# One fused transformer layer on one core: a sixth gate/up product ahead of the gate, the first query ahead of a cast, casts moved round a table load, and a twelfth split down

## The reference

```
x = x + xattn(layernorm(x), ctx_512)       # 16 heads, causal mask over the first 32 context rows
x = x + attn(layernorm(x))                 # 16 heads, q/k/v/o with LoRA of rank 16
x = x + ffn(layernorm(x))

def ffn(flat):                             # 128 x 256; E = 32 experts, I = 128, top 4
    scores = sqrt(softplus(flat @ router_w.T))
    _, idx = top_k(scores + expert_bias, 4)
    topv   = scores at idx, divided by their sum
    out = sum over all experts e of  p[:, e] * swiglu(flat, gate_w[e], up_w[e], down_w[e])
    return out + swiglu(flat, shared_gate_w, shared_up_w, shared_down_w)

def swiglu(x, wg, wu, wd):
    g = clip(x @ wg.T, -7, 7);  u = clip(x @ wu.T, -7, 7)
    return silu(g) * u @ wd.T
```

## Time and profile before

| | |
|---|---|
| three runs, us | 77.66, 73.18, 72.33 (median 73.18) |
| profiled execution, us | 72.22 |
| its span, first to last instruction, us | 70.4 |
| granted TensorE clock, mean | 1.000 |
| busy: TensorE, GpSimd, VectorE, ScalarE | 93%, 77%, 67%, 65% |
| HBM traffic | 15.52 MB read |

### The profile page before, as it was taken

The page is one execution under the profiler, slowest core; times in us unless marked ns, Lnnn a source line. Parts: engine busy times, 40 slices in busy tenths (PEclk is TensorE's granted clock), DMA queues, the critical chain, the costliest instruction groups (busy, mean ns, idle before and its releaser), DMA issues.

```text
span 70.4 us, 1578 instructions
## 1 busy us (share of the span) xinstructions
PE 65.3 (93%) x542; PEld 48.5 (69%) x542; DVE 47.0 (67%) x133; ACT 46.0 (65%) x101; POOL 54.2 (77%) x60
## 2 busy tenths in 40 slices
PE   5999989999799999999989999999999999999940
PEld 2348647789564496467666878888887888788820
DVE  0089488486497536499999945679955887697440
ACT  0606375876998654769979899999668851275220
POOL 7430003889999996998799999999999999999000
PEclk9999999999999999999999999999999999999999
DMA  0998999999999999999999995200000000000002
GB/s 3 271 297 245 329 425 404 291 328 419 417 419 403 393 401 407 396 383 388 393 407 400 391 372 201 76 0 0 0 9 0 0 0 0 0 0 0 0 0 74
DMA packets 6343, 15.75 MB, mean 224 GB/s; under 512 B 704, under 2 KB 1472, under 8 KB 6336
## 3 DMA queue, kind: packets, MB, share of 16 engines
q1 hardware_dynamic: 6048, 15.39, 59.2%
q10 hardware_dynamic: 288, 0.27, 1.1%
HBM read 15.52 MB, written 0.13 MB: 222 GB/s over the span
## 4 chain that ended last, share of the span: by engine, by line
PE 52%; DMA 16%; DVE 14%; SPq 7%; ACT 4%; issue 3%; DVEq 0%; ACTq 0%
DMA gu_raw<-moe_w_dram 16%; PE bP L591 16%; PE bY L624 7%; PE bY L613 6%; PE bXT L603 5%; SPq L275 4%; PE bE L591 4%; DVE gu_clip L964 4%; PE bY L626 3%; SPq L283 2%; DVE h L1018 2%; PE bP L419 2%; PE bXT L448 1%; PE bXT L641 1%; PE bY L444 1%
## 5 line engine op out<-in xcount | busy, mean ns | idle before, releaser
L349 POOL TENSOR_TENSOR gu_w<-gu_raw,gu_w 128x512 fp32r<-128x512 f32 x27 | 33.7, 1277 | 0.6 <-ACT gu_w L705 0.6
L591 PE MATMUL bP<-gu_w,xnT_parts 128*128 128x512 f32 x66 | 18.6, 417 | 0.0
L591 PEld LDWEIGHTS bP<-gu_w,xnT_parts 128*128 128x128 f32 x66 | 12.2, 188 | 2.9 <-issue 0.5
L1018 DVE SCALAR_TENSOR_TENSOR h<-gu_clip,gate,bP 128x128 f32<-128x128 f32 x26 | 7.8, 344 | 5.2 <-ACT bP L790 5.2
L964 DVE TENSOR_SCALAR gu_clip<-bP,clip_at 128x512 f32<-128x512 f32 x13 | 10.4, 806 | 1.1 <-PE bP L591 1.1
L355 POOL TENSOR_TENSOR gu_w<-dn_w,gu_w 128x512 fp32r<-128x512 f32 x8 | 10.1, 1285 | 0.0
L698 ACT ACTIVATE gu_w<-gu_raw 128x1024 fp32r<-128x1024 f32 x9 | 9.4, 1048 | 0.3 <-issue 0.3
L796 ACT ACTIVATE hT_parts<-bXT 128x256 fp32r<-128x256 f32 x11 | 4.2, 383 | 7.1 <-PE bXT L603 7.1
L705 ACT ACTIVATE gu_w<-gu_raw 128x512 fp32r<-128x512 f32 x10 | 6.1, 621 | 1.2 <-DMA gu_raw<-moe_w_dram 1.2
L603 PE MATMUL bXT<-consts_sb,h 128*128 128x128 f32 x33 | 6.5, 277 | 0.3 <-DVE h L1018 0.2
L790 ACT ACTIVATE bP<-gu_clip,rstd 128x256 f32<-128x256 f32 x13 | 6.1, 472 | 0.4 <-DVE gu_clip L964 0.4
(11 more groups left out here) (161 smaller groups left out, 124.8 us busy)
## 6 DMA issues: line engine op xcount, KB each, us to landing
gu_raw<-moe_w_dram SPq DMA_DIRECT2D x16, 512.0 KB, 9.6
dn_w<-moe_w_dram SPq DMA_DIRECT2D x16, 256.0 KB, 9.5
aw_sb<-attn_w_dram SPq DMA_DIRECT2D x2, 512.0 KB, 7.4
shared_sb<-shared_w_dram SPq DMA_DIRECT2D x1, 416.0 KB, 14.9
small_sb<-small_dram SPq DMA_DIRECT2D x1, 338.0 KB, 7.3
xwq_sb<-x_wq_dram SPq DMA_DIRECT2D x1, 256.0 KB, 3.5
lora_sb<-lora_dram SPq DMA_DIRECT2D x1, 256.0 KB, 4.7
ctx_sb<-ctx_kv_dram ACTq DMA_DIRECT2D x1, 192.0 KB, 3.2
```

What stands on the lines that cost most here:

```text
L349: nc.gpsimd.tensor_tensor(gu_w[:, gu_slot(p), 1, cols], gu_raw[:, raw_slot(p), cols], gu_w[:, gu_slot(p), 0, cols], ALU.subtract).then_inc ...
L591: last = nc.tensor.matmul(bGU[n % 5][:, 0:GU], xnT_parts[:, a, k, :], gu_w[:, gu_slot(n - 1), w, k * GU:(k + 1) * GU], start=(k == 0 and a ...
L1018: last = nc.vector.scalar_tensor_tensor(h[:, n % 4, e], gu_clip[:, n % 4, e, 1, :], weight_e, bank[:, e * 2 * I:e * 2 * I + I], ALU.mult, ...
```

## The change

Five edits, in one kernel.

1. **A sixth product ahead of the gate.** `BANKS` = 6: products 3 to 6 are issued before the first transposes, product 7 behind T(0). Product 6 gets the bank `bXT1` (`bOnce`). The routing scratch moves from there to `bShared`. Until unit 6 all transposes use the one bank `bXT0`, so `transpose_h(n)` waits for the copy of n - 1 and not of n - 2, and from the first split unit on for its low part as well. How far products are ahead is now `ahead(n)`: n + 6, from turn 5 on n + 5, from turn 8 on n + 4.
2. **Unit 0.** Its silu goes to the bank of unit 1 rather than the shared one, and `gate_h(0)` waits for silu 1.
3. **The first query of the second attention** is copied before the next cast rather than behind it, and the cast of pair 5 (counted from 0) is done in two halves, the second behind the copy of the probabilities.
4. **Casts round the table load.** The cast of pair 9 is done whole ahead of the table load; that of pair 10 in two halves behind silu 1. The copy of the leftover column moves up in the routing chain.
5. **Twelve split downs.** `LAST` = 12, `FIRST` = 4. A down cast is placed in the turn in which the product of its slot is issued.

```diff
+BANKS = 6
+LEADS = (5, 8)
-LAST = 11
+LAST = 12
+def ahead(n):
+    return min(n + BANKS - sum(n >= at for at in LEADS), PAIRS)
...
-        bHT = (bXT1, bXT0)
-        bGU = (bP[0][:, 0], bP[0][:, 1], bP[1][:, 0], bP[1][:, 1], bE)
+        bOnce = bXT1
+        def bGU(n):
+            if n == BANKS:
+                return bOnce
+            return (bP[0][:, 0], bP[0][:, 1], bP[1][:, 0], bP[1][:, 1], bE)[(n if n < BANKS else n - 1) % 5]
+        def bHT(n):
+            return bXT0 if n <= BANKS or n % 2 == 0 else bXT1
...
-                if n > 5:
-                    pe.wait_ge(h_ready, n - 4)
+                if n > BANKS:
+                    pe.wait_ge(h_ready, n - BANKS + (1 if n < 2 * BANKS else 2))
...
                 pe.wait_ge(h_ready, n + 1)
-                if n >= 2:
-                    pe.wait_ge(hT_ready, n - 1)
-                if n - 2 > FIRST:
-                    pe.wait_ge(hT_low_ready, n - 2 - FIRST)
+                back = 1 if n <= BANKS else 2
+                if n >= back:
+                    pe.wait_ge(hT_ready, n - back + 1)
+                if n - back > FIRST:
+                    pe.wait_ge(hT_low_ready, n - back - FIRST)
...
-            for n in range(WHOLE + 1, 6):
+            for n in range(WHOLE + 1, BANKS + 1):
                 gate_up(n)
             transpose_h(0, width=1)
+            gate_up(BANKS + 1)
             transpose_h(1)
             for n in range(2, PAIRS + 1):
-                if n + 4 <= PAIRS:
-                    gate_up(n + 4)
+                if ahead(n) > ahead(n - 1):
+                    gate_up(ahead(n))
                 transpose_h(n)
...
             for c in range(DC):
-                gu_high_chunk(WHOLE + 2, c)
                 act.wait_ge(q_psum, DC + c + 1)
                 nc.scalar.activation(qT[:, 1, c], ...)
+                gu_high_chunk(WHOLE + 2, c)
-            gu_high(WHOLE + 3)
+            gu_high_chunk(WHOLE + 3, 0)
...
             copy_probsT(1)
+            gu_high_chunk(WHOLE + 3, 1)
             gu_high(WHOLE + 4)
...
             nc.scalar.activation(root[:], half_power[:], ACT.Exp, scale=0.5).then_inc(root_ready, 1)
+            gu_high(WHOLE + 7)
             nc.scalar.preload_act_table(ACT.Silu)
...
-            gu_high_chunk(WHOLE + 7, 0)
             silu_unit(0)
             silu_unit(1)
-            gu_high_chunk(WHOLE + 7, 1)
-            gu_high(EARLY)
+            for c in range(DC):
+                gu_high_chunk(EARLY, c)
...
                 for i in range(UNITS, LAST):
-                    if dn_from(i) + 1 == n + 4:
+                    if ahead(n - 1) <= dn_from(i) < ahead(n):
                         dn_high(i)
```

More of the change, by code:

```diff
@@ L176, in build @@
         bLogits = bShared[:, 2 * I:SHARED]
-        logits_n, den, inv_root = (bXT1[:, at:at + E] for at in (64, 128, 192))
-        score2, weight = (bXT1[:, at:at + E + 1] for at in (256, 320))
-        bHT = (bXT1, bXT0)
+        logits_n, den, inv_root = (bShared[:, at:at + E] for at in (288, 320, 352))
+        score2, weight = (bShared[:, at:at + E + 1] for at in (384, 448))
         bLast = bP[0][:, 0]
-        bGU = (bP[0][:, 0], bP[0][:, 1], bP[1][:, 0], bP[1][:, 1], bE)
+        bOnce = bXT1
[5 more added lines that the diff above has]
+            return bXT0 if n <= BANKS or n % 2 == 0 else bXT1
         ld = {n: sem("ld_" + n) for n in ("x", "consts", "mask", "small", "ctx", "xwq", "lora", "rows", "aw_kq", "aw_vo", "shared")}
@@ L590, in gate_up @@
                         for a, w in HI_LO:
-                            last = nc.tensor.matmul(bGU[n % 5][:, 0:GU], xnT_parts[:, a, k, :],
+                            last = nc.tensor.matmul(bGU(n)[:, 0:GU], xnT_parts[:, a, k, :],
                                                     gu_w[:, gu_slot(n - 1), w, k * GU:(k + 1) * GU],
@@ L597, in transpose_h @@
                 pe.wait_ge(h_ready, n + 1)
-                if n >= 2:
-                    pe.wait_ge(hT_ready, n - 1)
-                if n - 2 > FIRST:
-                    pe.wait_ge(hT_low_ready, n - 2 - FIRST)
+                back = 1 if n <= BANKS else 2
[3 more added lines that the diff above has]
+                    pe.wait_ge(hT_low_ready, n - back - FIRST)
                 for e in range(width):
-                    last = nc.tensor.transpose(bHT[n % 2][:, e * T:(e + 1) * T], h[:, n % 4, e, :], ident)
+                    last = nc.tensor.transpose(bHT(n)[:, e * T:(e + 1) * T], h[:, n % 4, e, :], ident)
                 last.then_inc(hT_psum, 1)
@@ L619, in down @@
                     if n == PAIRS:
-                        pe.wait_ge(h_ready, PAIRS)
+                        pe.wait_ge(h_ready, PAIRS + 1)
                     for e in range(2):
@@ L782, in _ @@
             nc.scalar.activation(root[:], half_power[:], ACT.Exp, scale=0.5).then_inc(root_ready, 1)
+            gu_high(WHOLE + 7)
             nc.scalar.preload_act_table(ACT.Silu)
             def silu_unit(n):
-                act.wait_ge(clip_ready, n + 1)
+                act.wait_ge(clip_ready, max(n, 1) + 1)
                 width = 2 if n else 1
-                bank = bGU[n % 5] if n else bShared
-                dst = bank[:, 0:width * 2 * I].rearrange("p (e w i) -> p e w i", e=width, w=2)[:, :, 0, :]
+                dst = bGU(max(n, 1))[:].rearrange("p (e w i) -> p e w i", e=2, w=2)
+                dst = dst[:, :, 0, :] if n else dst[:, 0:1, 1, :]
                 nc.scalar.activation(dst, gu_clip[:, n % 4, 0:width, 0, :], ACT.Silu, scale=rstd[:, 2:3]
@@ L795, in hT_unit @@
                 dst = hT[:, n % 3, 0:width] if n <= FIRST else hT_parts[:, n % 3, 0]
-                nc.scalar.activation(dst, bHT[n % 2][:, 0:width * T], ACT.Copy).then_inc(hT_ready, 1)
+                nc.scalar.activation(dst, bHT(n)[:, 0:width * T], ACT.Copy).then_inc(hT_ready, 1)
             def dn_high(i):
@@ L956, in clip @@
                 width = 2 if n else 1
-                bank = bGU[n % 5] if n else bShared
+                bank = bGU(n) if n else bShared
                 if n:
@@ L976, in _ @@
             step(nc.vector.tensor_scalar(logits_n, bLogits, rstd[:, 2:3], None, ALU.mult))
+            dve.wait_ge(zeroed, 3)
+            step(nc.vector.tensor_copy(score2[:, E:E + 1], leftover[:]))
             dve.wait_ge(one_plus_ready, 1)
@@ L996, in _ @@
             step(nc.vector.tensor_tensor(inv_root, inv_root, softplus[:], ALU.mult))
-            dve.wait_ge(zeroed, 3)
-            step(nc.vector.tensor_copy(score2[:, E:E + 1], leftover[:]))
             step(nc.vector.tensor_tensor(score2[:, 0:E], inv_root, root[:], ALU.add))
@@ L1010, in gate_h @@
             def gate_h(n):
-                dve.wait_ge(silu_ready, n + 1)
+                dve.wait_ge(silu_ready, max(n, 1) + 1)
                 if n >= 4:
                     dve.wait_ge(hT_psum, n - 3)
-                bank = bGU[n % 5] if n else bShared
+                bank = bGU(max(n, 1))
+                at = 0 if n else I
                 for e in range(2 if n else 1):
@@ L1018, in gate_h @@
                     last = nc.vector.scalar_tensor_tensor(h[:, n % 4, e], gu_clip[:, n % 4, e, 1, :], weight_e,
-                                                          bank[:, e * 2 * I:e * 2 * I + I], ALU.mult, ALU.mult)
+                                                          bank[:, at + e * 2 * I:at + e * 2 * I + I], ALU.mult, ALU.mult)
                 last.then_inc(h_ready, 1)
@@ L1030, in hT_low @@
                 dve.wait_ge(hT_ready, n + 1)
[L1031 removed]
+                nc.vector.tensor_tensor(hT_parts[:, n % 3, 1], bHT(n)[:, 0:2 * T].rearrange("p (e t) -> p e t", e=2),
                                         hT_parts[:, n % 3, 0], ALU.subtract).then_inc(hT_low_ready, 1)
```

3 lines of the change are left out of this document (1 added, 2 removed).

## The result

| | before | after |
|---|---|---|
| median of 13 runs, us | 72.63 | 73.32 |
| lowest run, us | 71.97 | 72.42 |
| ratio, with its 95% interval | | 1.0114 [1.0081, 1.0147] |
| profiled execution and its span, us | 72.22, 70.4 | 73.35, 71.6 |

The ratio leaves disturbed executions out. As microseconds of the median before it is +0.83, between 0.59 and 1.07. The time lies in the predicted range, 0.9 us above the forecast, and the change that had been forecast as none is a small loss.

A forecast was written before the change was run, and what follows sets the result against it. A latency-bound front, then a TensorE-bound back from 37.57 us with ScalarE and GpSimd close behind. A lead of 1.47 us was lost in waits: 1.69 - 1.41 - 0.15 = +0.13 on 72.22, forecast 72.4 us, range 71.4 to 73.5.

The forecast's parts named there:

- the first query: Second attention: copying its first query ahead of the cast starts the scores earlier and shifts the front by 0.55 us.
- rival (c): Front: its gain is absent because a transfer or GpSimd holds the second query; 72.6 us, chance 0.08.
- at the load: ScalarE round the table load: whole cast 31.75 to 32.8, load to 34.1, h(1) near 35.7, taking back the front's gain.
- the forecast's +0.13: Net at the transposes of unit 6: 1.69 us later, less 1.41 for one more product and 0.15 for a cheaper down.
- T(6): TensorE's transposes of unit 6's gated activations: to wait 0.9 us for VectorE's low part of unit 5, starting at 48.74.
- T(5): TensorE's transposes of unit 5's gated activations: to wait 0.4 us for ScalarE's copy of unit 4, done at 45.08.
- The last column: Routing chain: moving this copy out saves one step, at most 0.2 us, taken at 0.2 and lost in the next step.
- Rival (d): Table load on ScalarE: costs its own 1.28 us once more behind a cast; 73.4 us, chance 0.04.
- ScalarE has no room behind the copy of unit 4: ScalarE in the back: three down casts in a row before silu 7, two of 0.52 us, delay the transposes of unit 6.
- the twelfth down: Split down 0.71 us against whole 0.86: TensorE gains 0.15; ScalarE gets one more cast, GpSimd one more subtraction.
- Rival (b): Back: landing of pair 12's transfer sets the time; a landing 1 us later gives 73.4 us, chance 0.17.
- Rival (a): Back: waits at the transposes of units 5 and 6 absent or small; GpSimd stops the gain at 0.7, 71.5 us, chance 0.15.

The follow-up runs named there:

- front_only: Kernel before with only the first query copied ahead of the casts and the cast of pair 5 in two halves; 72.38 us, ratio 0.9959 [0.9907, 1.0011].
- eleven_downs: Changed kernel with eleven split downs in place of twelve; 73.21 us, ratio to the kernel before 1.0057 [1.0009, 1.0106].
- before_again: Kernel before, unchanged, run and profiled a second time; 72.66 us, ratio 1.002 [0.999, 1.005].
- pair12_first: Changed kernel with the transfer of pair 12 issued ahead of those of 14, 15 and 13; 73.46 us, ratio to the kernel before 1.0104.
- table_and_down: Changed kernel with casts round the table load and turns of the down casts both as before; 72.68 us, ratio to the kernel before 0.9988.
- sixth_and_query: Changed kernel without the casts ahead of the table load, the earlier down casts and the twelfth split down; 72.25 us, ratio to before 0.988.

## Why the prediction was wrong

**The step that failed** is the first query: "The front shifts by 0.55 us up to the routing. The bounds are 0 (another wait takes its place) and 0.55; I take 0.55, since the row names the wait." The row named the wait of one execution, and even there the 0.55 was the idle time of the weight load: TensorE's key and query products would have let the scores start at 7.22 + 11.00 = 18.22, so it was worth 0.43. The wait is the difference of two arrivals, and both move from one execution to the next. The scores of the second attention come between 18.53 and 24.17 us, and the transfer, the first behind the issue of `bo_rows`, lands at 17.7 in both profiles of before, at 16.7 in front_only, 15.9 in the changed kernel and 18.4 in eleven_downs. When TensorE comes later or the transfer earlier, cast and transfer are done ahead of the query, and the edit removes a wait of nought: 0.02 us between before_again and pair12_first, no wait in the profile of front_only, 0.30 [-0.08, 0.68] over front_only's executions. What set the scores in its place was TensorE's own key and query products. In its effect this is rival (c), which I gave 0.08, though for another reason (there something was to hold the second query); its price, 0.38 us above 72.22, is too low by 0.48, most of it the term that follows.

**One more term was mis-sized**, at the load. The cast was to start when product 4 starts (32.27 there). Measured, with product 4 at 32.62, the cast starts at 32.90: the rows have product 3 from 31.39 for 1.40 us, to 32.79, past the start of product 4. From the scores to the cast I had 31.75 - 18.1 = 13.65 us; it took 13.94, 0.29 more, and the load, which waits for the whole of the cast as forecast, and the silus add 0.09. From the scores to h(1) I had 35.7 - 18.1 = 17.6 us; it took 36.94 - 18.96 = 17.98. That is 0.38 us, and it comes through the one chain that bounds the back now, ScalarE's.

**The sum with these two corrected:** scores without the gain, +0.55; h(1) later by 0.38; less the 0.28 us that I had ScalarE ahead of the cast of pair 12 (39.2 against 39.48), which now is spent. With the forecast's +0.13 that makes +0.78; the stretches differ by 0.86, the times by 0.83 [0.59, 1.07]. What is missing lies behind silu 7: from its start to T(6) the forecast has 48.74 - 46.53 = 2.21 us, the trace 49.81 - 47.48 = 2.33. With the measured stretch and the 0.31 us of the later start, 72.22 + 0.86 + 0.31 = 73.39 stands against the profiled 73.35. This takes edit 3 as worth nothing; with the 0.30 of front_only at its median the loss would be 0.56, just outside the interval.

**What was right.** The mechanism of the loss: T(6) was to wait 0.9 us for the low part of unit 5, near 48.7, and waits 0.96 us at 49.81 (30.6 us behind the scores forecast, 30.85 measured); T(5) 0.4, and TensorE's weight load idles 0.31 us there. The last column: from the scores to the root it is 31.58 - 18.65 = 12.93 us before, 31.72 - 18.96 = 12.76 after, so 0.17 for the 0.2 taken; it was lost, as said, since the cast waits for product 3 and not for the root. Rival (d) is out: load 1.28 us, silu 0.01 us behind, with a 1.06 us cast directly ahead. The Trainium skill (ScalarE: Activation LUTs, What ACT_TABLE_LOAD costs) has some 2.7 us with a drain; the row doesn't agree.

**What was half right.** That ScalarE has no room behind the copy of unit 4. I put all of it at the down casts; undoing the cast ahead of the load brings more (0.84 against 0.56 us), because it moves the whole chain of ScalarE, while the down casts move only its piece ahead of silu 7. And the twelfth down was to give 0.15 and gave 0.04: it saves TensorE 0.16 us, and makes T(6), which now waits for a low part, 0.20 us later. Rival (b), the landing of pair 12, wasn't the changed kernel's bound (pair12_first), but is that of one execution of the version in which ScalarE is early (1.10 us). Rival (a), GpSimd as the next bound at a gain of 0.7 us, is what table_and_down shows in its stretch once both reorderings are undone.

**The basis.** The sum was made against 72.22, a profile 0.4 us below its kernel's later median (72.63). The sign was there: the three times shown had their median at 73.18. I noted the gap and let it stand as a margin, where the question should have been what a slower execution does to each wait that the sum removes.

**Left open:** in what share of executions the first query waits before; whether edit 3 is worth 0 or some 0.3 us on average; why the landing of one transfer moves by 2.5 us between executions; and why table_and_down's shorter stretch shows so little in its times, beyond the 0.12 us behind it.

## What to carry to other kernels

A wait for a transfer that is read from one profile is the difference of two arrivals, that of the data and that of the compute, and here both moved by microseconds between executions. Before counting its removal as a gain, ask how long it is if the compute comes half a microsecond later or the data half a microsecond earlier. An engine with no slack behind a point (ScalarE here) is not the place to move work ahead of a fixed cost: the cast ahead of the table load waited 0.95 us for its slot and pushed load, silus and everything behind them. And when a change of five edits comes out even or worse, undo them one by one: here what was left of the change gained 0.7 us of the back with two reorderings of ScalarE undone, and these had cost 1.5, though the times of that kernel bear out only 0.1 and 0.9.

## What the runs showed of the hardware

- The first nine matmuls of one and the same program take 3.48 us in one execution and 4.00 in most (3.92 in eleven_downs), and the four key products behind them between 0.71 and 1.22 us, with a granted clock of 1.00 over the first 10 us in all fourteen profiles. That TensorE rose from its lower clock later in those executions is my reading of the durations and isn't shown: no row of the granted clock has a lower level there. The Trainium skill (TensorE: Matmul & The Clock Gate, Part 1: The HAM clock gate) has the moment of the change at around 4 us of matmuls and lets it differ by 500 ns either way from run to run. By that reading the 0.52 us could be such a difference, but the seven profiles of the last point below are outside it.
- The transfer of pair 12 landed 7.9 us behind its issue in the earlier trace rows, 6.4 in the changed kernel and 8.7 in sixth_and_query; the three of that stretch after 5.4 to 7.5 us in the changed kernel, and the four of sixth_and_query after 7.9 to 9.5. How long a transfer queues varies by more than the whole effect of this change.
- In seven profiles the first scores of the first attention all start at 9.68 us. The eight query products ahead of them, from 7.46 on, take 2.07 or 2.08 us; in the other seven profiles they take 1.15. Where their sixteen matmuls take 0.54 to 0.59 us (four profiles), the second attention's scores come at 20.8, where they take 0.68 (three), at 24.15 to 24.17; elsewhere they take 0.45. So the front varies by whole microseconds with TensorE's pace in it, while the back behind it repeats to 0.07 us.
